# First attention: all four exponent tiles added on GpSimd before the ones-matmul

## The chip, the cores and the metric

The kernel runs on one core of a Trainium2 chip. A core has five engines that work side by side, each with its own instruction stream: TensorE (PE, matrix products into the eight banks of PSUM), VectorE (DVE), ScalarE (ACT), GpSimd (POOL) and SyncE (SP, which issues transfers). They meet only through semaphores: an engine that waits for one does nothing else until it is reached, so whatever stands behind the waiting instruction waits too. The metric is the device time of one launch in microseconds (us).

## What is computed

Two decoder layers in float32 for x of shape (4, 512, 512): in each an attention, a mixing or cross attention, and a feed-forward part, with a layer norm behind each. The change touches only the first attention. Cut to that:

```python
positions = jnp.arange(s)
Q = (x @ W_q).reshape(b, s, 16, 32).transpose(0, 2, 1, 3)
K = (x @ W_k).reshape(b, s, 4, 32).transpose(0, 2, 1, 3)
V = (x @ W_v).reshape(b, s, 4, 32).transpose(0, 2, 1, 3)
Qr = _apply_rope(Q, positions)
Kr = _apply_rope(jnp.tile(K, (1, 4, 1, 1)), positions)
scores = jnp.einsum('bhqd,bhkd->bhqk', Qr, Kr) / 32 ** 0.5
weights = jax.nn.softmax(scores, axis=-1)
out = jnp.einsum('bhqk,bhkd->bhqd', weights, jnp.tile(V, (1, 4, 1, 1)))
x = _layernorm(x + out.transpose(0, 2, 1, 3).reshape(b, s, d) @ W_o)
```

Head h uses keys and values h mod 4. The softmax needs, for every head and query, the sum of 512 exponents.

## The kernel before

The function `rope_attention` is the first of five stages of the program and takes about 560 of its 2670 us. It works through four batches, and each batch through these parts: "project" (turn x, split it into a high and a low half, project to q, k, v with three passes), "keys" (turn the keys), "heads" (the attention of 16 heads) and "output" (multiply with W_o, layer norm). The function `turns` sets their order: heads of batch b, then project of batch b+1, then output of b, then keys of b+1. Every engine runs the same order. TensorE starts the project part of the next batch only when it has issued the whole heads part.

**The heads part.** A table `steps` sets the order on TensorE, ScalarE and VectorE. Head h has four steps "s" (scores of 128 queries, L660, whose row maximum VectorE takes at L594), a step "m" (turn the maxima, L668), and two head periods later four steps "e": the scores again, turned, so that keys lie on the partitions (L674). Before each head a step "q" turns its queries (L653). ScalarE takes the exponent of each "e" (L543) and writes it to `probsT[:, h % 6, k, :]`, a tile of 128 keys by 512 queries, k = 0 to 3. ScalarE also copies the turned queries and maxima (L532, L536).

**Groups of four heads.** Heads 4g to 4g+3 form group g, with four groups in a batch. Their products with v and their sums of exponents are made together. The pieces `("o", g, u, part)` stand in `steps` at fixed places; u is the half of the queries (256 columns). Parts 0 and 1 multiply exponents with v (L686). Part 2 makes the sums, in the same bank beside the products. In each piece head j of the group writes the partitions 32j to 32j+31, so that four narrow matmuls run side by side. The order of the pieces is (g,0,0), (g,0,1), (g,1,0), (g,0,2), (g,1,1), (g,1,2). The sum pieces are thus (g,0,2) and (g,1,2). VectorE takes the reciprocal (L580) and the quotient (L582), one quarter at a time, in steps "d".

**How the sums are made.** GpSimd adds three of the four exponent tiles of a head into `c.xcur[:, h % 4, :]`, an SBUF tile which this stage uses for nothing else. It takes two adds, L482 and L484, with a drain between. TensorE then multiplies the fourth tile and the sum with a block of ones, which adds over the partitions: 4 matmuls on `probsT` tile 3 and 4 on `xcur`, in each of the two sum pieces (L692). Before the first of them it waits until GpSimd has added all four heads of the group (semaphore `added`, L688).

**What GpSimd waits for.** There are four `xcur` slots, one for each head of a group. For head h of 4 and above GpSimd waits at L480 until the piece (g-1,1,2) has been issued and finished, that is until the sums of the group before are complete. It also waits for the exponents of its own head (L478).

**The end of a batch.** After the last exponents of head 15 no score matmuls are left to stand between the pieces. TensorE then issues all six pieces of group 3 in a row and goes on to turn x of the next batch (L620); the project part proper begins at L198. In the last batch there is no further project part: VectorE makes the last quotients (L580, L582) and TensorE goes on with the output (L705).

Of the kernel before, what the change touches and what calls it, by code (L numbers as in the profile page):

```python
# [20 lines left out]
P = 128  # L21
B, S, D = 4, 512, 512
T = S // P
KD = D // P
NH, HD, NKV = 16, 32, 4
# [317 lines left out]
def rope_attention(c):  # L343

    nc, d, ps = c.nc, c.d, c.ps
    with ExitStack() as ctx:
# [107 lines left out]
        @block.gpsimd  # L454
        def _(pool):
            pool.memset(kT[STK:P, :, :].bitcast(F32), 0.0)
            pool.drain()
            pool.memset(kT[STK:STK + 1, :, :].bitcast(F32), 1.0)
            pool.drain()
            pool.memset(nmax[:, :, :, :], 0.0).then_inc(frame, 1)  # L460

            pool.wait_ge(w_hi, 1)
            pool.drain()
            pool.tensor_tensor(wq_lo[:, 0:2, :], wraw[:, 0:2, :], wq_hi[:, 0:2, :].bitcast(F32), ALU.subtract).then_inc(w_lo, 1)  # L464

            def project(b, pos, heads_before):
                for t in range(T):

                    pool.wait_ge(*r_hi.after(b, t + 1))
                    rq = ra[:, t % 2, 0:D].rearrange("p (h e) -> p h e", e=HD)  # L470
                    rk = ra[:, t % 2, D:].rearrange("p (h e) -> p h e", e=HD)
                    pool.tensor_tensor(qs[:, t, :, 2 * HD:].bitcast(F32R), rq, qs[:, t, :, 0:HD], ALU.subtract)
                    pool.tensor_tensor(ks[:, t, :, HD:2 * HD].bitcast(F32R), rk, ks[:, t, :, 0:HD], ALU.subtract) \
                        .then_inc(stacked.sem, 1)

            def heads(b, pos):
                for h in range(NH):
                    pool.wait_ge(*ps.released(pos, ("e", h, 2)))  # L478
                    if h >= 4:
                        pool.wait_ge(*ps.full(pos, ("o", (h - 4) // 4, 1)))  # L480
                    p = [probsT[:, h % NPB, k, :] for k in range(3)]
                    pool.tensor_tensor(c.xcur[:, h % 4, :], p[0], p[1], ALU.add)  # L482
                    pool.drain()
                    pool.tensor_tensor(c.xcur[:, h % 4, :], c.xcur[:, h % 4, :], p[2], ALU.add).then_inc(added.sem, 1)  # L484

            def output(b, pos):
                c.pool_rstd(pool, b)

            turns(pool, project, nothing, heads, output)
# [120 lines left out]
        @block.tensor  # L610
        def _(pe):
            pe.wait_ge(first, 32)

            def project(b, pos, heads_before):
                if b > 0:
                    pe.wait_ge(x_in[b], 16)
                for k in range(KD):
                    ps.wait_empty(pe, pos, ("x", k))
                    for t in range(T):
                        mm = pe.transpose(ps.ap(("x", k))[:, t * P:(t + 1) * P],  # L620
                                          c.x[:, b * T + t, k * P:(k + 1) * P], c.ident[:, :])
                    mm.then_inc(ps.filled(("x", k)), 1)
                c.wait_xT(pe, pos)
                if b == 0:
                    pe.wait_ge(w_lo, 1)
                    pe.wait_ge(w_lo_dve, 1)
                    pe.wait_ge(frame, 1)
                for t in range(T):
                    ps.wait_empty(pe, pos, ("p", t))
                    for lo, hi, j in ((0, D, 0), (D, NQKV, 1)):  # L630
                        for k in range(KD):
                            mm = split3(pe, ps.ap(("p", t), j)[:, 0:hi - lo],
                                        (c.xhi[:, k, t * P:(t + 1) * P], c.xlo[:, k, t * P:(t + 1) * P]),
                                        (wq_hi[:, k, lo:hi], wq_lo[:, k, lo:hi]), k == 0, k == KD - 1)
                    mm.then_inc(ps.filled(("p", t)), 1)

            def keys(b, pos, heads_before):
                pe.wait_ge(*stacked.after(b, T))
                for g in range(NKV):
                    ps.wait_empty(pe, pos, ("k", g))  # L640
                    for t in range(T):
                        mm = pe.transpose(ps.ap(("k", g))[0:STK, t * P:(t + 1) * P], ks[:, t, g, :], c.ident[:, :])
                    mm.then_inc(ps.filled(("k", g)), 1)

            def heads(b, pos):

                pe.wait_ge(*v_out.after(b, 1))
                for s in steps:
                    if s[0] not in "od":
                        ps.wait_empty(pe, pos, s)  # L650
                    if s[0] == "q":
                        for t in range(T):
                            mm = pe.transpose(ps.ap(s)[0:STK, t * P:(t + 1) * P], qs[:, t, s[1], :], c.ident[:, :])  # L653
                        mm.then_inc(ps.filled(s), 1)
                    elif s[0] == "s":
                        h, t = s[1:]
                        if t == 0:

                            pe.wait_ge(*ps.released(pos, ("q", h)))
                        pe.matmul(ps.ap(s), qT[:, h % NQB, t * P:(t + 1) * P], kT[:, h % NKV, :],  # L660
                                  start=True, stop=True).then_inc(ps.filled(s), 1)
                    elif s[0] == "m":
                        h = s[1]

                        for t in (T - 2, T - 1):
                            pe.wait_ge(*ps.released(pos, ("s", h, t)))
                        for t in range(T):
                            mm = pe.transpose(ps.ap(s)[0:P - STK, t * P:(t + 1) * P], nmax[:, h % 2, t, :], c.ident[:, :])  # L668
                        mm.then_inc(ps.filled(s), 1)
                    elif s[0] == "e":  # L670
                        h, k = s[1:]
                        if k == 0:
                            pe.wait_ge(*ps.released(pos, ("m", h)))
                        pe.matmul(ps.ap(s), kT[:, h % NKV, k * P:(k + 1) * P], qT[:, h % NQB, :],  # L674
                                  start=True, stop=True).then_inc(ps.filled(s), 1)
                    elif s[0] == "o":
                        g, u, part = s[1:]
                        key, half = ("o", g, u), slice(u * 2 * P, (u + 1) * 2 * P)
                        if part == 0:
                            ps.wait_empty(pe, pos, key)  # L680
                        if part < 2:
                            for k in (2 * part, 2 * part + 1):
                                if u == 0:
                                    pe.wait_ge(*ps.released(pos, ("e", 4 * g + 3, k)))
                                for j in range(4):
                                    pe.matmul(ps.ap(key)[j * HD:(j + 1) * HD, 0:2 * P], v[:, k, j * HD:(j + 1) * HD],  # L686
                                              probsT[:, (4 * g + j) % NPB, k, half], start=(k == 0), stop=(k == T - 1))
                        else:  # L688
                            pe.wait_ge(*added.after(b, 4 * g + 4))
                            for k in range(2):  # L690
                                for j in range(4):
                                    mm = pe.matmul(ps.ap(key)[j * HD:(j + 1) * HD, 2 * P:4 * P], c.ones[:, 0:HD],  # L692
                                                   c.xcur[:, j, half] if k else probsT[:, (4 * g + j) % NPB, T - 1, half],
                                                   start=(k == 0), stop=(k == 1))
                            mm.then_inc(ps.filled(key), 1)

            def output(b, pos):
                if b == 0:
                    pe.wait_ge(wo_in, 16)
                for u in range(2):  # L700
                    pe.wait_ge(*ps.released(at("heads", pos[0]), ("o", NKV - 1, u)))
                for t in range(T):
                    ps.wait_empty(pe, pos, ("y", t))
                    for k in range(KD):
                        mm = pe.matmul(ps.ap(("y", t)), outT[:, k, t * P:(t + 1) * P], wo[:, k, :],  # L705
                                       start=(k == 0), stop=(k == KD - 1))
                    mm.then_inc(ps.filled(("y", t)), 1)

            turns(pe, project, keys, heads, output)
# [1958 lines left out]
```

## Time and profile before

| | us |
|---|---|
| median of three runs | 2669.71 |
| lowest and highest run | 2669.33, 2671.48 |
| time of the profiled execution | 2671.59 |
| its span, first to last instruction | 2669.8 |
| TensorE busy | 2235.3 |
| VectorE busy | 1415.9 |
| ScalarE busy | 1209.1 |
| GpSimd busy | 911.8 |

The profile holds one execution. The page gives each engine's busy time, a strip of 40 slices with the clock that TensorE was granted, and the costliest groups of instructions. The trace can be asked for a list in order of time, for one line's instructions, and for busy times in chosen stretches. Times in it count from the start of the span. TensorE's clock has two levels, 1.2 and 2.4 GHz; the column PEclk shows 0.50 and 1.00 for them. Matmuls are pipelined and their ends are modelled, so the distance between two starts says more than a duration. A float32 matmul leaves two records: "x8" of L692 are four matmuls.

### The profile page before, as it was taken

Reading aid. Unit: us, or ns where it says so; the run is one execution under the profiler, and the core shown is the slowest. Engines: PE = TensorE matmul, PEld = TensorE weight load, DVE = VectorE, ACT = ScalarE, POOL = GpSimd, SP = SyncE. Lnnn points to the kernel's source line nnn. Section 1 sums busy time; section 2 is a strip of 40 time slices with the busy share of each in tenths; the row PEclk is TensorE's granted clock in tenths of the full one; section 3 lists DMA queues with packets and bytes.
Section 4 is the critical chain, followed back from the end, with each engine's and each line's share of the span. In section 5 each row is a group of like instructions: output and inputs, shape, how many; then the busy total and the mean of one; then the engine's idle time right before and its main releaser. Section 6 shows DMA issues by size and latency. Waiting matters only on the chain. (4 is left out here: it accounts for less than half of the span.)

```text
span 2669.8 us, 35727 instructions
## 1 busy us (share of the span) xinstructions
PE 2235.3 (84%) x12406; PEld 1565.7 (59%) x12440; DVE 1415.9 (53%) x2138; ACT 1209.1 (45%) x2272; POOL 911.8 (34%) x570
## 2 busy tenths in 40 slices
PE   6888888857885887885999999999999999957672
PEld 4454545436674655553677767777777677734341
DVE  3656565634555335532555565556555755543445
ACT  3636363623424635442555545554555555522312
POOL 2424242410003202201455555555555455520101
PEclk8999898978997999997999999999999999978795
DMA  2000000010001000002111211121111011130001
GB/s 105 1 1 1 1 1 1 1 52 8 1 1 46 1 1 1 1 1 97 40 47 47 71 47 47 47 71 47 47 47 47 24 47 47 47 101 0 1 0 63
DMA packets 62365, 84.12 MB, mean 32 GB/s; under 512 B 6132, under 2 KB 41332, under 8 KB 61752
## 3 DMA queue, kind: packets, MB, share of 16 engines
q1 hardware_dynamic: 62264, 82.76, 9.2%
q8 instruction: 65, 1.06, 0.2%
q14 instruction: 36, 0.29, 0.0%
HBM read 74.36 MB, written 4.19 MB: 29 GB/s over the span
## 5 line engine op out<-in xcount | busy, mean ns | idle before, releaser
L1926 DVE RECIPROCAL s_inv_sums<-banks 128x512 f32<-128x512 f32 x64 | 214.8, 3357 | 343.2 <-PE banks L2039 339.8
L1800 POOL TENSOR_TENSOR s_qk_rstd<-s_mean_sq,minus_half 128x8 f32<-128x8 f32 x64 | 118.5, 1852 | 501.9 <-DVE s_mean_sq L1913 501.9
L594 DVE TENSOR_REDUCE s_neg_max<-banks 128x1 f32<-128x512 f32 x256 | 171.6, 688 | 113.6 <-PE banks L660 112.1
L2032 PE MATMUL banks<-s_probsT,s_v 128*128 128x512 f32 x512 | 230.9, 593 | 0.0
L1863 ACT ACTIVATE s_probsT<-banks,s_minus_bound,s_qk_rstd 128x512 f32<-128x512 f32 x256 | 177.0, 782 | 92.5 <-PE banks L200 88.5
L543 ACT ACTIVATE s_probsT<-banks 128x512 f32<-128x512 f32 x256 | 147.8, 599 | 100.5 <-PE banks L674 98.6
L198 PE MATMUL banks<-s_w_proj_hi,xT_hi 128*128 (+1 forms) x512 | 170.7, 333 | 2.9 <-DVE s_ctxT_lo L1974 2.9
L1834 ACT ACTIVATE s_squares<-banks 128x512 f32<-128x512 f32 x64 | 38.2, 597 | 284.0 <-PE banks L200 284.0
L2032 PEld LDWEIGHTS banks<-s_probsT,s_v 128*128 128x128 f32 x512 | 97.5, 190 | 111.0 <-issue 108.3
L1793 POOL TENSOR_TENSOR s_w_proj_lo<-s_w_proj_raw,s_w_proj_hi 128x2048 f32 (+1 forms) x33 | 152.0, 4606 | 14.4 <-ACT s_w_proj_hi L1826 14.4
L1809 POOL TENSOR_TENSOR s_probs_pair_sums<-s_probsT 128x1024 f32<-128x1024 f32 x64 | 151.0, 2360 | 7.2 <-issue 7.2
L660 PE MATMUL banks<-s_kT,s_qT 128*128 128x512 f32 x256 | 124.3, 491 | 29.8 <-ACT s_qT L532 16.2
L482 POOL TENSOR_TENSOR x_cur<-s_probsT 128x512 f32<-128x512 f32 x64 | 81.8, 1278 | 189.2 <-PE banks L692 111.6
L199 PE MATMUL banks<-s_w_proj_lo,xT_hi 128*128 (+1 forms) x512 | 145.7, 284 | 0.0
L200 PE MATMUL banks<-s_w_proj_hi,xT_lo 128*128 (+1 forms) x512 | 145.5, 284 | 0.0
L198 PE MATMUL banks<-s_wqkv_hi,xT_hi 128*128 128x512 f32 (+1 forms) x256 | 91.0, 355 | 34.6 <-POOL s_wqkv_lo L464 8.8
L674 PE MATMUL banks<-s_qT,s_kT 128*128 128x512 f32 x256 | 108.8, 431 | 4.8 <-ACT s_probsT L543 4.6
L198 PEld LDWEIGHTS banks<-s_w_proj_hi,xT_hi 128*128 128x128 f32 x512 | 98.8, 193 | 18.1 <-issue 18.1
L198 PE MATMUL banks<-s_w_out_hi,s_outT_hi 128*128 (+1 forms) x256 | 104.3, 407 | 5.8 <-DVE s_outT_lo L1933 5.8
L199 PEld LDWEIGHTS banks<-s_w_proj_lo,xT_hi 128*128 128x128 f32 x512 | 98.9, 193 | 14.8 <-issue 14.8
L198 PE MATMUL banks<-s_w_proj_hi,s_ctxT_hi 128*128 (+1 forms) x256 | 101.4, 396 | 7.1 <-ACT s_v L1849 7.1
L1959 DVE TENSOR_TENSOR x_all<-banks,x_all 128x512 f32 (+1 forms) x128 | 85.6, 689 | 35.6 <-PE banks L200 32.5
(412 smaller groups left out, 5949.5 us busy)
## 6 DMA issues: line engine op xcount, KB each, us to landing
s_w_proj_raw<-l1x_wq SPq DMA_DIRECT2D x33, 512.0 KB, 4.6
s_w_out_raw<-l1x_wo SPq DMA_DIRECT2D x33, 512.0 KB, 3.6
s_w_proj_raw<-l1x_wk SPq DMA_DIRECT2D x33, 256.0 KB, 4.8
s_w_proj_raw<-l1x_wv SPq DMA_DIRECT2D x33, 256.0 KB, 5.3
x_all<-x SPq DMA_DIRECT2D x4, 1024.0 KB, 13.0
s_ctxT<-ctxT SPq DMA_DIRECT2D x8, 512.0 KB, 6.0
x_cur<-x_all SPq DMA_DIRECT2D x4, 1024.0 KB, 7.6
out<-x_all SPq DMA_DIRECT2D x4, 1024.0 KB, 4.3
```

Source lines behind the costliest of these rows:

```text
L198: pe.matmul(out, lhs[0], rhs[0], start=start, stop=False)
L199: pe.matmul(out, lhs[0], rhs[1], start=False, stop=False)
L200: return pe.matmul(out, lhs[1], rhs[0], start=False, stop=stop)
L543: act.activation(probsT[:, h % NPB, k, :], ps.ap(s), ACT.Exp).then_inc(ps.freed(s), 1)
L594: dve.tensor_reduce(nmax[:, h % 2, t, 0:1], ps.ap(s), AX.X, ALU.max, negate=True) \
L660: pe.matmul(ps.ap(s), qT[:, h % NQB, t * P:(t + 1) * P], kT[:, h % NKV, :], start=True, stop=True).then_inc(ps.filled(s), 1)
L1793: pool.tensor_tensor(out, raw, hi.bitcast(F32), ALU.subtract).then_inc(done.sem, 1)
L1800: pool.tensor_tensor(rs[:, j, :, :], ms[:, j, :, :], c.mhalf[:, 0:T * HP].rearrange("p (t h) -> p t h", h=HP), ALU.pow) \
L1809: pool.tensor_tensor(psum2[:, :, :], probsT[:, h, 0:2, :], probsT[:, h, 2:4, :], ALU.add)
L1863: act.activation(probsT[:, h, k, :], pb.ap(("e", h, k)), ACT.Exp, bias=bound[:, 0:1], scale=rs[:, 1, k, h:h + 1]).then_inc(pb.freed(("e", ...
L1926: dve.reciprocal(inv[:, h, :], pb.ap(("sum", h))).then_inc(pb.freed(("sum", h)), 1)
L2032: mm = pe.matmul(pb.ap(("o", h)), v[:, k, h * DX:(h + 1) * DX], probsT[:, h, k, :], start=(k == 0), stop=(k == T - 1))
```

## The change

GpSimd waits for the fourth exponent tile of a head instead of the third, and adds it too, with a further drain and a third add of the same size. TensorE leaves out the four matmuls on the fourth tile in each sum piece. Everything else is as before.

```diff
                 for h in range(NH):
-                    pool.wait_ge(*ps.released(pos, ("e", h, 2)))
+                    pool.wait_ge(*ps.released(pos, ("e", h, T - 1)))
                     if h >= 4:
                         pool.wait_ge(*ps.full(pos, ("o", (h - 4) // 4, 1)))
-                    p = [probsT[:, h % NPB, k, :] for k in range(3)]
+                    p = [probsT[:, h % NPB, k, :] for k in range(T)]
                     pool.tensor_tensor(c.xcur[:, h % 4, :], p[0], p[1], ALU.add)
                     pool.drain()
-                    pool.tensor_tensor(c.xcur[:, h % 4, :], c.xcur[:, h % 4, :], p[2], ALU.add).then_inc(added.sem, 1)
+                    pool.tensor_tensor(c.xcur[:, h % 4, :], c.xcur[:, h % 4, :], p[2], ALU.add)
+                    pool.drain()
+                    pool.tensor_tensor(c.xcur[:, h % 4, :], c.xcur[:, h % 4, :], p[3], ALU.add).then_inc(added.sem, 1)
...
                             pe.wait_ge(*added.after(b, 4 * g + 4))
-                            for k in range(2):
-                                for j in range(4):
-                                    mm = pe.matmul(ps.ap(key)[j * HD:(j + 1) * HD, 2 * P:4 * P], c.ones[:, 0:HD],
-                                                   c.xcur[:, j, half] if k else probsT[:, (4 * g + j) % NPB, T - 1, half],
-                                                   start=(k == 0), stop=(k == 1))
+                            for j in range(4):
+                                mm = pe.matmul(ps.ap(key)[j * HD:(j + 1) * HD, 2 * P:4 * P], c.ones[:, 0:HD],
+                                               c.xcur[:, j, half], start=True, stop=True)
                             mm.then_inc(ps.filled(key), 1)
```

The first place is the end of a batch's heads part on TensorE. Before (L686 are products with v, L692 the sum pieces, L620 turns x of the next batch):

```order
L674 MATMUL banks<-s_qT,s_kT 128x512 x7
L686 MATMUL banks<-s_probsT,s_v 32x256 x24
L692 MATMUL banks<-s_probsT,ones_sb 32x256 x4
L692 MATMUL banks<-x_cur,ones_sb 32x256 x4
L686 MATMUL banks<-s_probsT,s_v 32x256 x8
L692 MATMUL banks<-s_probsT,ones_sb 32x256 x4
L692 MATMUL banks<-x_cur,ones_sb 32x256 x4
L620 MATMUL banks<-ident_sb,x_all 128x128 x16
```

The same place in the changed kernel, whose lines stand two further down from there on (L688 for L686, L693 for L692, L622 for L620):

```order
L676 MATMUL banks<-s_qT,s_kT 128x512 x7
L688 MATMUL banks<-s_probsT,s_v 32x256 x24
L693 MATMUL banks<-x_cur,ones_sb 32x256 x4
L688 MATMUL banks<-s_probsT,s_v 32x256 x8
L693 MATMUL banks<-x_cur,ones_sb 32x256 x4
L622 MATMUL banks<-ident_sb,x_all 128x128 x16
```

The four matmuls on `probsT` have gone from each sum piece; the order of what is left is the same.

The second place is GpSimd's own stream at the turn from head 3 to head 4 of a batch, with what each instruction waits for. Before:

```order
L482 TENSOR_TENSOR x_cur<-s_probsT 128x512 [waits bank2_freed]
L484 TENSOR_TENSOR x_cur<-x_cur,s_probsT 128x512
L482 TENSOR_TENSOR x_cur<-s_probsT 128x512 [waits bank7_filled,bank2_freed]
L484 TENSOR_TENSOR x_cur<-x_cur,s_probsT 128x512
L482 TENSOR_TENSOR x_cur<-s_probsT 128x512 [waits bank7_filled,bank2_freed]
```

In the changed kernel:

```order
L482 TENSOR_TENSOR x_cur<-s_probsT 128x512 [waits bank3_freed]
L484 TENSOR_TENSOR x_cur<-x_cur,s_probsT 128x512
L486 TENSOR_TENSOR x_cur<-x_cur,s_probsT 128x512
L482 TENSOR_TENSOR x_cur<-s_probsT 128x512 [waits bank7_filled,bank3_freed]
L484 TENSOR_TENSOR x_cur<-x_cur,s_probsT 128x512
L486 TENSOR_TENSOR x_cur<-x_cur,s_probsT 128x512
```

Each head has a third add. The wait for the exponents has moved from bank 2 (tiles 0 and 2) to bank 3 (tiles 1 and 3); the wait on bank 7, which is the sum piece of the group before, is as it was.

## Rows read from the trace of the kernel before

**Rows 1.** Stretches (start:end, us; PE, PEld, DVE, ACT, POOL busy; PEclk): heads, then project.
```profile
54.00:145.00 91.00, 80.14 (x639) 46.20 (x638) 54.76 (x86) 52.48 (x95) 40.75 (x32) 0.94 0.00 1
145.00:188.00 43.00, 36.98 (x171) 25.07 (x168) 27.41 (x49) 13.00 (x31) 7.85 (x9) 1.00 0.00 1
```

**Rows 2.** One line's instructions, L692: records of the matmuls on the fourth tile.
```profile
L692 PE MATMUL banks<-s_probsT,ones_sb x256: 379/379/403, 80.2 to 542.6; 128*32 128x256 f32 x128
...
  POOL x_cur L482: 111.6, 12
```

**Rows 3.** In order of time (start, us, engine, line), batch 0: first sum piece of group 2.
```profile
124.09 0.64 PE L692 MATMUL banks<-s_probsT,ones_sb 128*32 128x256 f32 x8
...
124.55 0.61 PE L692 MATMUL banks<-x_cur,ones_sb 128*32 128x256 f32 x8
...
125.63 0.69 DVE L594 TENSOR_REDUCE s_neg_max<-banks 128x1 f32<-128x512 f32 x1 [0.97 <-PE banks L660]
```

**Rows 4.** In order of time, batch 0: GpSimd's first heads, and group 0's sum piece.
```profile
62.89 1.27 POOL L482 TENSOR_TENSOR x_cur<-s_probsT 128x512 f32<-128x512 f32 x1 [16.63 <-ACT s_probsT L543]
...
63.18 0.62 ACT L543 ACTIVATE s_probsT<-banks 128x512 f32<-128x512 f32 x1
...
66.59 1.28 POOL L482 TENSOR_TENSOR x_cur<-s_probsT 128x512 f32<-128x512 f32 x1 [0.99 <-ACT s_probsT L543]
...
80.22 0.64 PE L692 MATMUL banks<-s_probsT,ones_sb 128*32 128x256 f32 x8
```

**Rows 5.** In order of time, GpSimd, batch 0: it resumes after group 1's sum pieces.
```profile
107.17 1.29 POOL L482 TENSOR_TENSOR x_cur<-s_probsT 128x512 f32<-128x512 f32 x1 [9.69 <-PE banks L692]
108.60 1.28 POOL L484 TENSOR_TENSOR x_cur<-x_cur,s_probsT 128x512 f32<-128x512 f32 x1
109.84 1.28 POOL L482 TENSOR_TENSOR x_cur<-s_probsT 128x512 f32<-128x512 f32 x1
```

**Rows 6.** In order of time, batch 0: GpSimd's resumption for group 3; TensorE to the project part.
```profile
129.10 1.28 POOL L482 TENSOR_TENSOR x_cur<-s_probsT 128x512 f32<-128x512 f32 x1 [9.67 <-PE banks L692]
...
141.78 0.60 PE L692 MATMUL banks<-s_probsT,ones_sb 128*32 128x256 f32 x8
142.21 0.60 PE L692 MATMUL banks<-x_cur,ones_sb 128*32 128x256 f32 x8
142.64 1.04 PE L686 MATMUL banks<-s_probsT,s_v 128*32 128x256 f32 x16
...
144.47 1.09 PE L620 MATMUL banks<-ident_sb,x_all 128*128 128x128 f32 x8
...
149.52 0.47 PE L198 MATMUL banks<-s_wqkv_hi,xT_hi 128*128 128x512 f32 x1 [1.72 <-DVE xT_lo L299]
```

**Rows 7.** In order of time, batch 1: the same two moments of group 3.
```profile
261.21 1.28 POOL L482 TENSOR_TENSOR x_cur<-s_probsT 128x512 f32<-128x512 f32 x1 [9.65 <-PE banks L692]
...
269.80 4.79 PE L686 MATMUL banks<-s_probsT,s_v 128*32 128x256 f32 x48
274.41 0.60 PE L692 MATMUL banks<-s_probsT,ones_sb 128*32 128x256 f32 x8
```

**Rows 8.** Stretches, columns as above: the stage start and the ends of batches.
```profile
45.19:58.85 13.66, 11.05 (x40) 7.92 (x40) 4.49 (x7) 4.16 (x7) 1.07 (x2) 0.50 0.00 0
130.53:133.94 3.41, 1.30 (x7) 0.62 (x6) 3.26 (x6) 2.00 (x5) 3.27 (x3) 1.00 0.00 0
133.94:140.77 6.83, 6.42 (x37) 2.97 (x41) 1.51 (x4) 3.21 (x6) 5.58 (x5) 0.50 0.01 2
144.18:149.50 5.32, 2.64 (x24) 1.70 (x17) 2.92 (x5) 2.28 (x4) 0.00 (x0) 1.00 0.00 0
543.54:546.95 3.41, 0.05 (x1) 0.08 (x1) 3.04 (x6) 0.00 (x0) 0.00 (x0) 1.00 0.00 0
546.95:550.37 3.42, 3.42 (x4) 1.38 (x5) 0.00 (x0) 0.00 (x0) 0.00 (x0) 0.50 0.00 0
```

**Rows 9.** In order of time, TensorE, last batch: the output begins.
```profile
546.90 5.37 PE L705 MATMUL banks<-s_wo,s_outT 128*128 128x512 f32 x8 [3.47 <-issue]
```

## The prediction

> **What bounds the kernel now.** I read the page first, then the stretches of the first stage, then the order of time around the sum pieces. The page's busy times (the table above) are averages over five stages. In the heads part of batch 0 TensorE works 80.1 of 91 us and GpSimd 40.8, and in the project part behind it TensorE works 37.0 of 43 [rows 1]. So TensorE bounds this stage nearly everywhere. Its one weak place is the end of a batch, where it waits for exponents: 1.30 us of work in 3.41 us [rows 8].
>
> GpSimd seems to have room. It sat idle 111.6 us, 12 times, until a sum piece was done [rows 2]. This idle time is the trap of the case. It lies *before* GpSimd may start on a group, because the four slots of the sum are still read. What counts is the time from that start to the moment when TensorE wants the result. I call this the window of a group. Its two ends stand in [rows 3, 5 to 7].
>
> **What TensorE saves.** The removed matmuls number 128: 4 in each of 32 sum pieces [rows 2]. In the middle of a batch the first half of a piece takes 124.55 - 124.09 = 0.46 us [rows 3]. Is it on the path? VectorE was idle 0.97 us, until the scores right behind this piece came [rows 3]. So it can take them 0.46 earlier, and the whole chain moves up. At the end of a batch the half takes 142.21 - 141.78 = 0.43 [rows 6]. In the last batch the second half there is hidden behind the quotients, which start from the first piece and keep TensorE waiting afterwards [rows 9]. Sum: 24 x 0.46 + 7 x 0.43 = 11.0 + 3.0 = **14.0 us saved**, if nothing comes late.
>
> **What GpSimd needs now.** An add starts 1.43 us after the one before it in the same head (108.60 - 107.17, drain included), and the next head starts 1.24 after that [rows 5]. No row shows the third add, but it has the size, the operands in SBUF and the drain of the second. Its price lies between 1.24 (no drain seen) and 1.43; I take 1.43, since it depends on the add before it as the second does. A head goes from 1.43 + 1.24 = 2.67 us to 1.43 + 1.43 + 1.24 = 4.10, and four heads in a row take 3 x 4.10 + 1.43 + 1.43 + 1.28 = 16.44 us. With a little for the semaphore's way I take **16.5 us a group**.
>
> **Group 0.** GpSimd now waits for the fourth exponent, which ends at 63.18 + 0.62 = 63.80 [rows 4], not the third. The next heads' exponents come 66.59 - 62.89 = 3.70 us apart [rows 4], faster than 4.10, so GpSimd falls behind from the first head on. It is done at 63.8 + 16.5 = 80.3, where TensorE wants it at 80.22 [rows 4]. That is a wait of about 0.1 us, four times: **0.4 us lost**.
>
> **Groups 1 and 2.** Here the window is 124.09 - 107.17 = 16.92 us [rows 3, 5], against 16.5. Nothing that the change removes lies inside a window, so it stays as long as it was. GpSimd is just in time, with some 0.4 us to spare, and all of the saving stands. What would cost: if a head took 4.21 instead of 4.10, the cover would be gone.
>
> **Group 3.** The window is shorter, since no score matmuls of further heads stand in it: 141.78 - 129.10 = 12.68 us in batch 0 [rows 6] and 274.41 - 261.21 = 13.20 in batch 1 [rows 7]. TensorE has to wait 16.5 - 12.68 = 3.82 and 16.5 - 13.20 = 3.30. With the mean of these, 3.56, for all four batches the sum is **14.2 us lost**. Queued behind this wait on TensorE are the last product piece, the last sum piece, the turning of x, and the whole project part. ScalarE and VectorE can't help: both are idle until TensorE turns x. In the last batch the quotients and the output wait. I find no work in the trace that covers any of it.
>
> Without the clock the sum is 14.2 + 0.4 - 14.0 = **+0.6 us**: the swap just about pays for its own stall.
>
> **The clock.** A gap of some microseconds in TensorE's work has been followed by the low clock here. After 1.30 us of work in 3.41 the clock was 0.50, which is 1.2 GHz, for 6.83 us [rows 8]. After the pause of 3.47 us before the output [rows 9] it was 0.50 for 3.42 us [rows 8]. The new wait is a pause of the same length, at a place where TensorE now runs at 2.4 GHz: from 144.18 on PEclk is 1.00, though TensorE works there only 2.64 of 5.32 us [rows 8]. What a low clock costs is seen in the product pieces. In batch 1 the 48 records from 269.80 to 274.41 take 4.61 us [rows 7], while 16 of them take about 0.87 at 2.4 GHz (142.64, to the sum piece behind it) and 48 would take 2.6.
>
> Now the part behind the wait, in batch 0. It resumes at 145.6. The last three pieces, 0.43 + 0.87 + 0.43 = 1.7 us at 2.4 GHz, cost up to 1.7 more. The turning of x takes 149.52 - 144.47 = 5.05 us [rows 6] with two runs of eight transposes, which cost about 1.1 more together. Then the project part begins, where every microsecond at 1.2 GHz costs half a microsecond. If the low clock lasts 6.83 us, it covers the pieces and the first transposes, for 2.2 us. If it lasts 13.66, as once at the start of the stage [rows 8], it reaches some 3 us into the project part and costs 1.7 + 1.1 + 1.7 = 4.5. I take 3.4 for the first three batches, between these, and 1.0 for the last, where the quotients hide most: 3 x 3.4 + 1.0 = **11.2 us**. The lower end of this term is 0, the upper about 20, when the clock falls twice in a batch.
>
> The Trainium skill ("TensorE: Matmul & The Clock Gate", section "Why this matters for your kernels") advises against pauses between bursts of matmuls in mid kernel, since the clock goes back to its low level behind them. By that rule every batch would pay this term; if it didn't hold here, the sum would be the +0.6. The trace's two pauses go with the rule. The same page, in its part on PE-mode transposes, says that transposes don't hold the clock up; the stretch 144.18:149.50, half of it transposes and pauses, stayed at 1.00, so here the trace doesn't bear that out.
>
> **The sum.** +0.6 + 11.2 = +11.8 us on the profiled execution's 2671.6, which is 2683.4, or 0.44%. The profiled execution lies 1.9 above the median of the runs, 2669.7, and what surrounds the span (1.8 us) doesn't change. On the median the forecast is 2669.7 + 11.8 = **2681.5 us**.
>
> **Rivals.**
> - *The stall comes, the clock doesn't follow*, or is back before the project part. For: the wait may be split so that TensorE works before and behind it, and at 144.18 a half-idle stretch did no harm. Against: both pauses of over 2 us did [rows 8]. Time: 2669.7 + 0.6 = 2670.3, up to 2675 with part of the term.
> - *The wait at a batch's end is covered after all* (the faster side). Something in the project part waits for another engine anyway and takes the delay up. It would decide from 3.6 us of such slack in each batch. For: TensorE is idle 6 of 43 us there [rows 1]. Against: this idle time is the chain TensorE, ScalarE, VectorE around the turning of x, which moves as one piece. Time: 2669.7 - 14.0 + 0.4 = 2656.1.
> - *GpSimd is slower than I think and groups 1 and 2 wait too*. From 4.21 us a head on each of 8 more pieces is late. With 4.3 us a head a group takes 0.8 us more: 8 x 0.38 there and 8 x 0.8 in groups 0 and 3, 9 us more: 2691. Against: its adds last 1.27 to 1.29 us in all rows [rows 4 to 7].
> - *The change doesn't do what it says*: it does, the four matmuls are gone from each piece and the third add is there, so it gets no chance.
>
> **How the numbers follow.** Stall and clock, 2675 to 2690: 0.68. Stall alone: 0.20. GpSimd slower still: 0.08. Covered wait: 0.04. The range of 2670 to 2692 holds the first three nearly whole and leaves out the covered wait and the far end of the clock term. A measurement of this kernel can tell about 0.2%, 5.3 us, from no change. Slower by more than that is the first case and the third with a little of the second: 0.78. Within it: 0.18. Faster: 0.04.
>
> **What would show it.** In the profile after, GpSimd's three adds should start 1.43 us apart and a group take 16.5 us. The piece (3,0,2) should start 16.5 us after GpSimd's first add of the group, with TensorE idle for 3.3 to 3.9 us just before it, released by GpSimd, in all four batches. In groups 1 and 2 no such wait should stand, and the two sum pieces of a group should stand 0.46 us closer to each other. PEclk behind the wait should read 0.50 for 3 to 14 us. I would be wrong if TensorE's wait there is under 2 us, if it is as long and the project part begins no later, or if PEclk stays at 1.00.

## The result, and the profile after

| | us |
|---|---|
| before, median of 13 runs (lowest to highest) | 2669.33 (2666.66 to 2671.80) |
| changed, median of 13 runs (lowest to highest) | 2675.46 (2670.29 to 2681.31) |
| ratio, with its 95% interval | 1.0023 (1.0015 to 1.0032) |

The change makes the kernel 6.1 us slower, and the runs now lie 11 us apart instead of 5. The profiled execution took 2675.46 us, with a span of 2673.6.

The page of the changed kernel, busy times by engine:

```profile
PE 2226.2 (83%) x12184; PEld 1558.8 (58%) x12184; DVE 1415.6 (53%) x2138; ACT 1208.5 (45%) x2272; POOL 991.3 (37%) x634
```

GpSimd has 64 more instructions and 80 us more work. TensorE has 9 us less, and still the span is longer. So what counts is not how much the engines work but when, and at what clock. In order of time, batch 0, GpSimd on the first head of group 2 and TensorE's two sum pieces of group 1 (start, us, engine, line):

```profile
101.63 0.64 PE L693 MATMUL banks<-x_cur,ones_sb 128*32 128x256 f32 x8
...
104.97 0.64 PE L693 MATMUL banks<-x_cur,ones_sb 128*32 128x256 f32 x8
...
105.78 1.29 POOL L482 TENSOR_TENSOR x_cur<-s_probsT 128x512 f32<-128x512 f32 x1 [4.75 <-ACT s_probsT L545]
107.21 1.28 POOL L484 TENSOR_TENSOR x_cur<-x_cur,s_probsT 128x512 f32<-128x512 f32 x1
108.63 1.28 POOL L486 TENSOR_TENSOR x_cur<-x_cur,s_probsT 128x512 f32<-128x512 f32 x1
109.86 1.29 POOL L482 TENSOR_TENSOR x_cur<-s_probsT 128x512 f32<-128x512 f32 x1
```

These answer to [rows 3, 5]. The adds start 1.43, 1.42 and 1.23 us apart, so a head takes 4.08 us instead of 2.67. The idle time in front of GpSimd was 9.69 us [rows 5] and is 4.75. (The profile now names ScalarE for it, whose exponents had long been there; the start still follows the sum piece directly.) There is no wait before either sum piece. The sum pieces gave back what the removed matmuls took: the distance of the groups on GpSimd is 126.84 - 105.78 = 21.06 us, and was 129.10 - 107.17 = 21.93 [rows 5, 6].

The end of the batch, in order of time, batch 0, with GpSimd's first add of group 3:

```profile
126.84 1.28 POOL L482 TENSOR_TENSOR x_cur<-s_probsT 128x512 f32<-128x512 f32 x1 [4.71 <-ACT s_probsT L545]
...
143.13 0.64 PE L693 MATMUL banks<-x_cur,ones_sb 128*32 128x256 f32 x8 [3.81 <-POOL x_cur L486]
143.59 1.05 PE L688 MATMUL banks<-s_probsT,s_v 128*32 128x256 f32 x16
144.45 0.62 PE L693 MATMUL banks<-x_cur,ones_sb 128*32 128x256 f32 x8
145.00 1.09 PE L622 MATMUL banks<-ident_sb,x_all 128*128 128x128 f32 x8
...
150.04 0.47 PE L198 MATMUL banks<-s_wqkv_hi,xT_hi 128*128 128x512 f32 x1 [1.72 <-DVE xT_lo L299]
```

They answer to [rows 6]. TensorE waits 3.81 us for GpSimd, and then everything runs as before: the turning of x takes 5.04 us again. A like wait stands at the end of the other batches. Batches 1 to 3, in order of time:

```profile
275.43 1.08 PE L693 MATMUL banks<-x_cur,ones_sb 128*32 128x256 f32 x8 [3.22 <-POOL x_cur L486]
276.29 1.93 PE L688 MATMUL banks<-s_probsT,s_v 128*32 128x256 f32 x16
...
279.01 1.97 PE L622 MATMUL banks<-ident_sb,x_all 128*128 128x128 f32 x8
...
284.77 0.77 PE L198 MATMUL banks<-s_wqkv_hi,xT_hi 128*128 128x512 f32 x1 [1.72 <-DVE xT_lo L299]
...
412.53 0.64 PE L693 MATMUL banks<-x_cur,ones_sb 128*32 128x256 f32 x8 [3.68 <-POOL x_cur L486]
...
543.87 1.08 PE L693 MATMUL banks<-x_cur,ones_sb 128*32 128x256 f32 x8 [5.83 <-POOL x_cur L486]
```

Two of the four batches show something more: behind the waits of 3.22 and 5.83 us the sum pieces last 1.08 instead of 0.64, and the product piece 1.93 instead of 1.05. That is the low clock. By stretch (start:end, length, busy PE, PEld, DVE, ACT, POOL, then PEclk), before and behind the waits:

```profile
143.13:150.04 6.91, 4.21 (x48) 2.65 (x49) 2.94 (x5) 2.28 (x4) 0.00 (x0) 1.00 0.01 2
270.89:274.30 3.41, 1.33 (x24) 0.48 (x16) 0.00 (x0) 0.00 (x0) 3.12 (x4) 1.00 0.00 0
274.30:281.13 6.83, 5.54 (x40) 2.96 (x40) 0.34 (x1) 0.71 (x2) 1.08 (x1) 0.50 0.01 2
284.54:287.95 3.41, 3.18 (x8) 2.54 (x9) 3.19 (x6) 0.00 (x0) 0.00 (x0) 0.50 0.00 0
412.53:419.44 6.91, 4.21 (x48) 2.66 (x49) 2.94 (x5) 2.28 (x4) 0.00 (x0) 1.00 0.01 2
540.54:547.37 6.83, 3.50 (x32) 1.38 (x32) 2.20 (x4) 0.00 (x0) 2.99 (x3) 0.50 0.00 0
550.78:554.19 3.41, 3.41 (x6) 1.35 (x5) 0.00 (x0) 0.00 (x0) 0.00 (x0) 0.50 0.02 5
```

In batches 0 and 2 the clock stayed at 2.4 GHz behind a wait of 3.7 to 3.8 us. In batch 1 it fell at 274.30, some 1.1 us before the wait's end, after a stretch in which TensorE had worked 1.33 of 3.41 us. It was at 1.2 GHz for 6.83 us and, behind the pauses of the turning of x, for 3.41 more. In batch 3 it fell 3.3 us before the wait's end, for 6.83 us. So the same kind of wait costs differently from batch to batch. The length of the wait doesn't decide it: 3.81 us left the clock up and 3.22 us didn't.

### The profile page after: what moved, and what is told of

It reads as the page before. It is cut to its first block and busy times, and to the rows that moved or that the text cites. A ratio compares the mean times of both kernels' runs of the same rounds, so it can differ in the third digit from the quotient of the medians.

```text
span 2673.6 us, 35377 instructions
## 1 busy us (share of the span) xinstructions
PE 2226.2 (83%) x12184; PEld 1558.8 (58%) x12184; DVE 1415.6 (53%) x2138; ACT 1208.5 (45%) x2272; POOL 991.3 (37%) x634
## 5 line engine op out<-in xcount | busy, mean ns | idle before, releaser
L662 PE MATMUL banks<-s_kT,s_qT 128*128 128x512 f32 x256 | 122.8, 485 | 30.2 <-ACT s_qT L534 16.5
L199 PEld LDWEIGHTS banks<-s_w_proj_lo,xT_hi 128*128 128x128 f32 x512 | 99.1, 193 | 14.8 <-issue 14.8
```

Source lines behind the costliest of these rows:

```text
L199: pe.matmul(out, lhs[0], rhs[1], start=False, stop=False)
```

## The experiments

The theory has four parts: a saving of 0.43 us in each of 31 sum pieces; a wait of 3.2 to 3.8 us at each batch's end (5.8 where TensorE comes early), since GpSimd may only start on group 3 when the sums of group 2 are done; a low clock behind some of these waits; and nothing anywhere else. The experiments take the parts away one by one. Each gives its time against the kernel before, run beside it.

**The two halves apart.** The first keeps TensorE's old sum pieces and has only GpSimd's third add (the diff is against the changed kernel):

```diff
-                            for j in range(4):
-                                mm = pe.matmul(ps.ap(key)[j * HD:(j + 1) * HD, 2 * P:4 * P], c.ones[:, 0:HD],
-                                               c.xcur[:, j, half], start=True, stop=True)
+                            for k in range(2):
+                                for j in range(4):
+                                    mm = pe.matmul(ps.ap(key)[j * HD:(j + 1) * HD, 2 * P:4 * P], c.ones[:, 0:HD],
+                                                   c.xcur[:, j, half] if k else probsT[:, (4 * g + j) % NPB, T - 1, half],
+                                                   start=(k == 0), stop=(k == 1))
```

> GpSimd's half of the change alone: it adds all four exponent tiles, while TensorE still makes the eight matmuls of each sum piece, so the fourth tile is counted twice in the sums. My theory: the change is a saving of 31 x 0.43 = 13.3 us, a wait in group 3 of 14.4 us in all, 0.4 us in group 0, and some 5 us of low clock behind the waits. Without the saving that is 2669.3 + 20 = 2689 us (2685 to 2694), with TensorE waiting 3.2 to 5.8 us for GpSimd in each batch. Rival (saving and wait are both half as large, and there is no clock term): 2679.

Measured: 2693.95 us against 2668.28, ratio 1.0099 (1.0083 to 1.0114), 25.7 us slower. The time is just inside the range I gave (up to 2694), but the difference isn't: the upper end stood for 24.7 us above the kernel before, and I had expected 20. TensorE's waits are there, in order of time, batches 0 to 2:

```profile
143.28 1.08 PE L694 MATMUL banks<-s_probsT,ones_sb 128*32 128x256 f32 x8 [3.43 <-POOL x_cur L486]
...
282.75 1.08 PE L694 MATMUL banks<-s_probsT,ones_sb 128*32 128x256 f32 x8 [3.07 <-POOL x_cur L486]
...
422.33 1.08 PE L694 MATMUL banks<-s_probsT,ones_sb 128*32 128x256 f32 x8 [5.85 <-POOL x_cur L486]
```

In batch 3 the wait is 5.84 us. All four are followed by pieces at the low clock (1.08 us), and in batches 1 to 3 the clock fell a second time a few us later. The four waits of this trace add up to 18.2 us, but two of them are long only because TensorE came early. Against the 14.8 us of waits in my sum that leaves 11 us. I put them down to the clock, since each wait has double the work in the sum pieces behind it and the clock was low behind all four; but this is a subtraction, and no run measures the term by itself. The rival (2679) is out.

The second experiment has TensorE's half alone (the diff is against the kernel before):

```diff
-                            for k in range(2):
-                                for j in range(4):
-                                    mm = pe.matmul(ps.ap(key)[j * HD:(j + 1) * HD, 2 * P:4 * P], c.ones[:, 0:HD],
-                                                   c.xcur[:, j, half] if k else probsT[:, (4 * g + j) % NPB, T - 1, half],
-                                                   start=(k == 0), stop=(k == 1))
+                            for j in range(4):
+                                mm = pe.matmul(ps.ap(key)[j * HD:(j + 1) * HD, 2 * P:4 * P], c.ones[:, 0:HD],
+                                               c.xcur[:, j, half], start=True, stop=True)
```

> TensorE's half alone: the four matmuls on the fourth tile are left out of each sum piece and GpSimd adds three tiles as before, so the fourth tile is missing from the sums. My theory: 2669.3 - 13.3 = 2656 us (2653 to 2658), no wait for GpSimd anywhere. Rival (half of the saving hides behind other engines): 2662.5.

Measured: 2656.67 us, ratio 0.9955 (0.9941 to 0.9969), 11.6 us faster. The 13.3 lie inside the interval (8 to 16 us); the 6.8 that half hidden matmuls would give (2662.5 against 2669.3) lie outside. TensorE waits for GpSimd nowhere in the stage. Batch 0, all its waits (us in total, times, longest):

```profile
PE banks L660 <- ACT s_qT L532: 3.5, 7, 0.6
PE banks L668 <- DVE s_neg_max L594: 2.3, 3, 1.3
PE banks L660 <- DVE s_neg_max L594: 2.0, 2, 1.0
PE banks L198 <- DVE xT_lo L299: 1.8, 1, 1.8
PE banks L686 <- DVE s_outT L582: 1.8, 2, 0.9
PE banks L674 <- ACT s_probsT L543: 1.4, 4, 0.8
PE banks L620 <- DVE xT_lo L299: 1.0, 1, 1.0
```

**The clock alone.** The changed kernel, with work that nobody needs put into the wait:

```diff
                         else:
+                            if g == NKV - 1 and u == 0:
+                                for i in range(13):
+                                    pe.matmul(ps.ap(("m", NH - 1)), qT[:, i % NQB, 0:P], kT[:, g, :], start=True, stop=True)
                             pe.wait_ge(*added.after(b, 4 * g + 4))
```

> The changed kernel, with 13 matmuls of 512 columns (about 3 us at 2.4 GHz) on TensorE before the wait of group 3, whose results nobody reads. They fit into the wait of 3.2 to 3.8 us, so the wait's end stays where GpSimd puts it; TensorE only doesn't rest. My theory (the clock behind the wait costs some 5 us in the mean of runs): 2670 to 2672 us, and no fall of the clock within 7 us behind the wait. Rival (the low clock costs nothing here, the 6 us come from the wait itself): 2675.5, as the changed kernel.

Measured: 2671.05 us against 2668.28, ratio 1.0010 (1.0001 to 1.0019), 2.8 us slower. In order of time, batch 0 (L693 here is the added work), and the stretches from the added work to the project part in batches 0 to 2:

```profile
136.28 3.25 PE L693 MATMUL banks<-s_kT,s_qT 128*128 128x512 f32 x13
140.28 0.64 PE L696 MATMUL banks<-x_cur,ones_sb 128*32 128x256 f32 x8 [0.75 <-POOL x_cur L486]
```

```profile
137.00:147.20 10.20, 6.75 (x61) 4.41 (x59) 2.96 (x5) 2.28 (x4) 2.94 (x3) 1.00 0.01 2
269.50:279.60 10.10, 7.21 (x62) 4.78 (x61) 2.98 (x5) 2.28 (x4) 2.81 (x3) 1.00 0.00 1
402.70:412.80 10.10, 6.99 (x62) 4.60 (x60) 2.97 (x5) 2.28 (x4) 2.82 (x3) 1.00 0.00 0
```

The wait's end stays where GpSimd puts it, only 0.75 us of rest are left, and the clock stays up in all three. To see how far the changed kernel's own figure moves, it was run again on another chip, beside the next experiments:

> The changed kernel once more, beside the next three on the same chip. My theory and its rival both say what was measured: 5 to 7 us above the kernel before, with a spread of some 10 us between its runs, since the clock falls behind the waits in some batches of a run and not in others.

Measured: 2676.59 us against 2667.50, ratio 1.0034 (1.0021 to 1.0046), 9.1 us slower, 2673.7 to 2681.3 in six runs. Here the clock was low behind the waits of batches 1 and 2. In order of time, the end of the wait and the start of the project part in these two:

```profile
272.99 1.08 PE L693 MATMUL banks<-x_cur,ones_sb 128*32 128x256 f32 x8 [3.27 <-POOL x_cur L486]
...
282.33 0.77 PE L198 MATMUL banks<-s_wqkv_hi,xT_hi 128*128 128x512 f32 x1 [1.72 <-DVE xT_lo L299]
...
408.22 1.08 PE L693 MATMUL banks<-x_cur,ones_sb 128*32 128x256 f32 x8 [5.86 <-POOL x_cur L486]
...
416.83 0.47 PE L198 MATMUL banks<-s_wqkv_hi,xT_hi 128*128 128x512 f32 x1 [1.72 <-DVE xT_lo L299]
```

The changed kernel thus stands 6.1 and 9.1 us above the kernel before, and 2.8 with the wait filled. **The low clock costs 3 to 6 us**, and the wait against the saving leaves about 3. These are differences between medians from different chips, and the 2.8 alone has an interval of 0.3 to 5.1. The two traces of the changed kernel bear the size out. From the wait's end to the project part a batch takes 6.91 us at the high clock. Batch 1 took 9.34 in both traces, 2.4 more, and then had some 3.1 us of the project part at half speed, which costs about 1.6 more. Batch 2 of the second trace took 8.61, 1.7 more. In batch 3 of the first trace the fall cost 0.5 us up to the output (6.36 us, and 5.82 with the wait filled). Up to the last batch's output that makes 4.5 us in the first trace and 5.7 in the second.

**The place of the loss.** The change in groups 0 to 2, the old way in group 3 (the diff is against the changed kernel, and so are those of the next three):

```diff
-                    pool.wait_ge(*ps.released(pos, ("e", h, T - 1)))
+                    last = h >= NH - 4
+                    pool.wait_ge(*ps.released(pos, ("e", h, T - 2 if last else T - 1)))
...
-                    pool.drain()
-                    pool.tensor_tensor(c.xcur[:, h % 4, :], c.xcur[:, h % 4, :], p[2], ALU.add)
-                    pool.drain()
-                    pool.tensor_tensor(c.xcur[:, h % 4, :], c.xcur[:, h % 4, :], p[3], ALU.add).then_inc(added.sem, 1)
+                    for k in range(2, T - 1 if last else T):
+                        pool.drain()
+                        add = pool.tensor_tensor(c.xcur[:, h % 4, :], c.xcur[:, h % 4, :], p[k], ALU.add)
+                    add.then_inc(added.sem, 1)
...
-                            for j in range(4):
-                                mm = pe.matmul(ps.ap(key)[j * HD:(j + 1) * HD, 2 * P:4 * P], c.ones[:, 0:HD],
-                                               c.xcur[:, j, half], start=True, stop=True)
+                            first = 0 if g == NKV - 1 else 1
+                            for k in range(first, 2):
+                                for j in range(4):
+                                    mm = pe.matmul(ps.ap(key)[j * HD:(j + 1) * HD, 2 * P:4 * P], c.ones[:, 0:HD],
+                                                   c.xcur[:, j, half] if k else probsT[:, (4 * g + j) % NPB, T - 1, half],
+                                                   start=(k == first), stop=(k == 1))
```

> The change in groups 0 to 2 of each batch, the old way (three adds, eight matmuls) in group 3, so the result is the whole computation. My theory: all of the loss sits in group 3; 24 x 0.43 = 10.3 us are saved and 0.4 lost in group 0: 2659.5 us (2657 to 2662), no wait for GpSimd in group 3. Rival (three adds a head cost something in groups 0 to 2 too, by late groups or by shared ports): 2664 to 2669.

Measured: 2656.79 us against 2668.28, ratio 0.9959 (0.9946 to 0.9973), 11.5 us faster than the kernel before. The 10 us expected lie inside the interval (7.2 to 14.4). The loss sits in group 3: with that group as it was, the rest of the change only gains. In order of time, batch 0, TensorE goes from the product pieces to the sum pieces with no wait (in batch 3 it waits 0.30 us, elsewhere not at all):

```profile
134.00 4.17 PE L689 MATMUL banks<-s_probsT,s_v 128*32 128x256 f32 x48
138.00 0.60 PE L696 MATMUL banks<-s_probsT,ones_sb 128*32 128x256 f32 x8
138.43 0.60 PE L696 MATMUL banks<-x_cur,ones_sb 128*32 128x256 f32 x8
```

This version computes the same and beats both kernels. It was run once more on another chip:

> The version with the old way in group 3 once more, on the same chip: 10 to 12 us below the kernel before, as the first time. Rival (the first time's gain was the chip or the phase of the clock): 5 us or less.

Measured: 2656.80 us against 2668.42, ratio 0.9951 (0.9938 to 0.9964), 11.6 us faster.

**What opens the window.** Groups 1 and 3 get slots of their own, in buffers that are free in the heads part:

```diff
+        def slot(h):
+            if h // 4 % 2 == 0:
+                return c.xcur[:, h % 4, :]
+            return (ra[:, 0, 0:S], ra[:, 1, 0:S], rb[:, 0:S], v_next.ap().rearrange("p t n -> p (t n)"))[h % 4]
...
-                    if h >= 4:
-                        pool.wait_ge(*ps.full(pos, ("o", (h - 4) // 4, 1)))
+                    if h >= 8:
+                        pool.wait_ge(*ps.full(pos, ("o", (h - 8) // 4, 1)))
```

with `slot(h)` in place of `c.xcur[:, h % 4, :]`.

> The changed kernel with eight slots for the sums instead of four (groups 1 and 3 use buffers that are free in the heads part), so that GpSimd no longer waits for the sum pieces of the group before. Theory (the window is opened by that wait): GpSimd starts on head 12 when its exponents are there, finishes group 3 about 1.4 us earlier against TensorE's arrival, and is held only by the exponents of the last heads, which come faster than 4.1 us apart; the wait of group 3 shrinks from 3.2 to 3.8 us to about 2.3, and the kernel is 5 to 8 us faster than the changed one, about the time of the kernel before. Rival (the wait comes from GpSimd's speed on the last head alone, not from a late start): no difference to the changed kernel.

Measured: 2666.73 us against 2667.50, ratio 0.9998 (0.9990 to 1.0007); against the changed kernel on the same chip (2676.59) 9.9 us faster, somewhat more than expected. TensorE's waits before the first sum piece of group 3, batches 0 to 3:

```profile
141.47 0.41 PE L698 MATMUL banks<-s_rope_a,ones_sb 128*32 128x256 f32 x2 [2.00 <-POOL s_v_next L491]
...
272.78 0.64 PE L698 MATMUL banks<-s_rope_a,ones_sb 128*32 128x256 f32 x2 [3.82 <-POOL s_v_next L491]
...
408.02 0.41 PE L698 MATMUL banks<-s_rope_a,ones_sb 128*32 128x256 f32 x2 [2.31 <-POOL s_v_next L491]
...
538.72 0.64 PE L698 MATMUL banks<-s_rope_a,ones_sb 128*32 128x256 f32 x2 [3.81 <-POOL s_v_next L491]
```

Two of them are 2.0 and 2.3 us, as expected. The other two are 3.8. In those the trace has no low clock before the product pieces (in batches 0 and 2 it is low there from 131.15 and 400.80 on), so TensorE came earlier to its wait. The four waits add up to 11.9 us and were 16.5. The profiled execution took 2672.41 us, among the longest of the eleven, so its waits need not be the typical ones. The rival, that the late start doesn't matter, is out by the times. A shorter wait was no protection from the low clock: in this trace it came behind all four waits, behind the 2.0 us of batch 0 too, from 148.22 on, where the project part begins (148.38). What brought it down there is not shown.

**What is queued behind the wait.** The last product piece is put ahead of the sum piece that waits:

```diff
+                if g == NKV - 1 and piece in (("o", g, 0, 2), ("o", g, 1, 1)):
+                    piece = ("o", g, 1, 1) if piece[2] == 0 else ("o", g, 0, 2)
```

> The changed kernel with the last product piece of group 3 (0.87 us) put ahead of the sum piece that waits. Theory (what is queued behind the wait is lost one for one): the wait is 0.87 us shorter in each batch and its end stays where it was; 3.5 us below the changed kernel, up to 5 with some clock. Rival (the wait's place in the order doesn't matter, since something else holds the next part back): no difference.

Measured: 2672.38 us against 2667.50, ratio 1.0016 (1.0007 to 1.0024); 4.2 us below the changed kernel on the same chip, where 3.5 to 5 were expected. The intervals of the two just touch (1.9 to 6.4 and 5.6 to 12.3 us above the kernel before), so the size is rough. Batches 0 and 1, in order of time:

```profile
141.66 1.07 PE L695 MATMUL banks<-x_cur,ones_sb 128*32 128x256 f32 x16 [2.59 <-POOL x_cur L488]
...
273.69 1.07 PE L695 MATMUL banks<-x_cur,ones_sb 128*32 128x256 f32 x16 [1.99 <-POOL x_cur L488]
```

The waits are 1.22 and 1.23 us shorter (3.81 and 3.22 in the changed kernel), where the piece at 2.4 GHz is 0.87. Their end stayed with GpSimd, 16.3 us after its start on the group. The clock was low for 3.41 us in the project parts behind batches 0 to 2 of this trace, so the 4.2 us are not the waits alone.

**How much room groups 1 and 2 have.** A small add behind each head's third:

```diff
+                    pool.tensor_tensor(pad[:, :], c.ones[:, 0:64], c.ones[:, 64:P], ALU.add)
```

> The changed kernel with one more small add of 128x64 elements on GpSimd behind each head's third, on data nobody uses, some 0.3 us each. Theory (groups 1 and 2 have only 0.4 us to spare): a group takes 17.7 us instead of 16.4, TensorE waits 0.7 to 0.8 us in groups 1 and 2, and 1.2 us more in groups 0 and 3; 8 x 0.75 + 8 x 1.2 = 15 to 16 us above the changed kernel. Rival (groups 1 and 2 have room): 8 x 1.2 = 9 to 10 us above it.

Measured: 2688.53 us against 2667.50, ratio 1.0081 (1.0066 to 1.0095), 11.9 us above the changed kernel, between theory and rival. The expectation had a slip: the small add of the last head comes after its signal, so that a group grows by three of them, not four. TensorE's waits in batch 0, groups 0, 1 and 2:

```profile
79.83 0.64 PE L695 MATMUL banks<-x_cur,ones_sb 128*32 128x256 f32 x8 [0.88 <-POOL x_cur L487]
...
101.24 0.64 PE L695 MATMUL banks<-x_cur,ones_sb 128*32 128x256 f32 x8 [0.26 <-POOL x_cur L487]
...
122.64 0.64 PE L695 MATMUL banks<-x_cur,ones_sb 128*32 128x256 f32 x8 [0.26 <-POOL x_cur L487]
```

A group now waits 0.26 us where none waited, with less than 0.9 us more work on GpSimd (three adds, each 0.29 from its start to the next head's). So the room was about 0.6 us, a little more than the 0.4 of the prediction, whose group took 16.5 us where 16.3 were measured.

**The clock before the wait.** In the version with the old last group, as in the kernel before, TensorE also rests between the last exponent matmuls, and the product pieces behind run at 1.2 GHz. Seven matmuls that nobody needs, one behind each of these (the diff is against the version with the old last group):

```diff
+                        if h == NH - 1 or (h == NH - 2 and k > 0):
+                            pe.matmul(ps.ap(("s", NH - 1, 0)), kT[:, h % NKV, 0:P], qT[:, h % NQB, :], start=True, stop=True)
```

> The version with the old way in group 3, and seven matmuls of 512 columns whose results nobody reads, one behind each of the last seven exponent matmuls of a batch, where TensorE waits for ScalarE. Theory (the clock falls there because TensorE rests, and the product pieces behind it then run at 1.2 GHz for 3 to 4 us, which costs half of that): the clock stays up there, 1.5 to 2 us saved in each batch, 6 to 8 us below the version without them. Rival (the added matmuls delay the exponents as much as the clock gains): no difference, or slower by up to 7 x 0.23 us in each batch.

Measured: 2654.89 us against 2668.42, ratio 0.9957 (0.9941 to 0.9973), six runs from 2651.85 to 2665.36. Beside it the version without the matmuls had 2656.80 and 0.9951 (0.9938 to 0.9964). This is inconclusive: the intervals cover each other. In batch 0 the clock did what the theory says: the 48 records of the product pieces now take 2.9 us (132.50 to 135.41) where the version without took 4.0 (134.00 to 138.00):

```profile
132.50 2.80 PE L691 MATMUL banks<-s_probsT,s_v 128*32 128x256 f32 x48
135.41 0.64 PE L698 MATMUL banks<-s_probsT,ones_sb 128*32 128x256 f32 x8
```

But the low clock turned up later in the same batch instead, from 142.31 on for 6.83 us, and the medians differ by 1.9 us, a quarter of what was expected. Whether there is a filling that keeps it up throughout stays open.

## Why the prediction was right, point by point

It said 2681.5 us, 2670 to 2692, slower. The time is 2675.5, on the forecast side and inside the range; the likeliest value was 6 us too high. The place, the cause and the length of the wait were right. The clock term was some two to three times too large.

- **The saving.** I had 0.46 us in the middle of a batch; the groups moved together by 21.93 - 21.06 = 0.87, so it is 0.43 to 0.44 a piece, and 13.3 in all instead of 14.0. TensorE's half alone gave 11.6 (8 to 16). Right, slightly large.
- **GpSimd's third add.** Forecast 1.43 us from start to start, measured 1.42; a group from 126.84 to TensorE's resumption at 143.13 takes 16.3 us, forecast 16.5. Right.
- **Groups 0 to 2.** No wait in groups 1 and 2. In group 0 of batch 0 GpSimd ended at 80.52 us and the sum piece began at 80.57, with no idle time in the trace, so a wait there is too short to show; 0.1 us was forecast. The version with the old group 3 shows that nothing is lost there, and the small add shows how thin the cover is.
- **Group 3.** Forecast 3.82 and 3.30 us in batches 0 and 1, measured 3.81 and 3.22. That the first agrees to 0.01 us is luck: the group took 0.2 us less than forecast, and TensorE was there 12.5 us after GpSimd's start instead of 12.7. Batch 3 has 5.83, since the clock hadn't fallen before the product pieces this time and TensorE came earlier; the end of the wait is GpSimd's in any case: the wait is longer there by what the product pieces had saved.
- **The cover.** What is queued behind the wait is lost one for one: with the wait's end the whole rest moved (the turning of x takes 5.04 us, and took 5.05), and moving one piece ahead shortened the waits by 1.2 us in the two batches shown and gave some 4 us back over the kernel.
- **The sum without the clock.** Forecast +0.6 us; with the wait filled it was 2.8 (0.3 to 5.1). The two don't contradict each other, but if the 2.8 is right, the sum was 2 us too low and hid a part of the clock term's excess.
- **The clock: the step that failed.** The sign was right, the size wasn't: 3 x 3.4 + 1.0 = 11.2 us forecast, 3 to 6 measured. I let the clock fall in every batch, from two pauses in the trace before. The runs show a wait of 3.7 to 3.8 us in batches 0 and 2 behind which PEclk stayed at 1.00, which the prediction had named as a sign of being wrong. The cost of one fall was nearly right: in batch 1 the stretch from the wait's end to the project part took 284.77 - 275.43 = 9.34 us, where batch 0 took 6.91, and the first 3.2 us of the project part were at half speed, which costs some 1.6 more. That makes 4.0 us, where 3.4 was forecast. (In the longer of its two cases the prediction let the low clock reach 3 us into the project part; its own numbers give 4. This moves the term by less than 1 us.) Half of 11.2, for a fall in every second batch, would have come within 1 us of the time, though partly since the +0.6 beside it was low.
- The rule of the Trainium skill on pauses between bursts ("TensorE: Matmul & The Clock Gate", "Why this matters for your kernels") held in direction, as the filled wait shows. By its wording every one of these waits should have brought the clock down; two of four did in the profiled run.

## What to carry to other kernels

Idle time of an engine is room only if it lies between the moment it may start and the moment its result is wanted. So measure that window at every place where the work stands, the last group of a loop above all: it is short, because the work that separated producer and consumer in the steady state has run out. When work is moved to an engine that fits in the steady state but not at the end, move it there and leave the end as it was: here that turned 6 to 9 us of loss into 11.5 us of gain.

## What the runs showed of the hardware

- A new pause on TensorE costs twice: once as such, and then, in some batches only, in the speed of what follows. Behind the four waits the clock was low in two batches in each of the two traces of the changed kernel. It stayed up at waits of 3.68 to 3.84 us (four of them) and fell at those of 3.22 and 3.27 and at the two of over 5.8.
- The spread of the runs doesn't tell such a pause by itself. It went from 5 to 11 us with the change and was 7 with the wait filled, but the version with the old last group and seven filling matmuls, which has no wait for GpSimd at all, had 13.5 us over six runs.
- On GpSimd an add of 128x512 elements in float32 lasted 1.28 us. From its start to the next one's it was 1.42 to 1.43 us with a drain between and 1.23 without; an add of 128x64 took 0.32.
- The stretch from the wait's end to the project part has three short pieces and then transposes with pauses between, and the clock stayed at 2.4 GHz in it (143.13:150.04, 4.21 of 6.91 us busy). In batch 1 it had risen during the transposes and fell again at their end (284.54).
- Two halves of a change needn't add up: 25.7 slower and 11.6 faster make 14.1, while the change measured 6.1 and 9.1. By the subtraction above the clock term is 11 us in the one half and 3 to 6 in the whole; that this is the reason is argued, not shown.
